# Two first pairs of the hidden folds leave the rank-2 projection for w2: five batches in place of six

## What is computed

```
xn = layernorm(x)
s  = weighted sum of shifted copies of xn (top 6 lags of each row's autocorrelation, softmax)
w1, w3: 2752 x 1024, each a 2752 x 256 matrix repeated four times along its columns; w2: 1024 x 2752, 1024 x 688 repeated likewise
gate = silu(xn w1' + 0.5 (xn a1') b1')      a1, b1 ... of rank 2
up   =      xn w3' + 0.5 (xn a3') b3'
hid  = gate * up                            4096 x 2752
y    = hid w2' + 0.5 (hid a2') b2'          a2: 2 x 2752, b2: 1024 x 2
out  = x + s * silu(y)
```

## Time and profile before

| | before |
|---|---|
| median of 3 runs | 848.47 us (848.42 to 848.81) |
| the profiled execution | 847.11 us, of which the span is 845.3 us |
| PE busy | 828.8 us, 98% of the span |
| DVE busy | 578.0 us, 68% |
| ACT busy | 332.1 us, 39% |
| POOL busy | 146.4 us, 17% |
| chain that ended last, PE's share | 90% |
| mean granted TensorE clock | 0.998 |

### The profile page before, as it was taken

The page is one execution under the profiler, slowest core; times in us unless marked ns, Lnnn a source line. Parts: engine busy times, 40 slices in busy tenths (PEclk is TensorE's granted clock), DMA queues, the critical chain, the costliest instruction groups (busy, mean ns, idle before and its releaser), DMA issues.

```text
span 845.3 us, 11238 instructions
## 1 busy us (share of the span) xinstructions
PE 828.8 (98%) x4200; PEld 440.2 (52%) x4200; DVE 578.0 (68%) x941; ACT 332.1 (39%) x544; POOL 146.4 (17%) x238
## 2 busy tenths in 40 slices
PE   5999999999999999999999999999999999999997
PEld 4434575336844367434763347534575336844366
DVE  7878734686767776688667776678766686744535
ACT  5987644434133342333423333333323334122231
POOL 5233102222012220122201230023201222000000
PEclk9999999999999999999999999999999999999999
DMA  9730035000230003200041010511014000220004
GB/s 292 268 109 26 26 126 199 26 26 26 100 125 26 26 26 125 100 26 26 27 160 65 26 30 22 200 30 45 26 51 175 26 1 0 101 100 1 1 2 149
DMA packets 18903, 62.13 MB, mean 73 GB/s; under 512 B 2464, under 2 KB 4224, under 8 KB 18576
## 3 DMA queue, kind: packets, MB, share of 16 engines
q1 hardware_dynamic: 18832, 61.28, 21.0%
HBM read 44.49 MB, written 16.78 MB: 72 GB/s over the span
## 4 chain that ended last, share of the span: by engine, by line
PE 90%; DVE 3%; ACT 2%; issue 2%; DVEq 1%; DMA 1%; POOL 0%; SPq 0%; ACTq 0%; POOLq 0%
PE g L1237 26%; PE u L1237 24%; PE zb L1397 5%; PE g L1456 4%; PE u L1456 4%; PE u L1465 4%; PE g L1465 4%; PE u L1463 4%; PE g L1463 4%; PE g L1285 3%; PE mb L1322 1%; DMA xf<-in_x 1%; PE g L1459 1%; PE u L1459 1%; DVE junk L797 1%
## 5 line engine op out<-in xcount | busy, mean ns | idle before, releaser
L539 ACT ACTIVATE sil<-g,winv 128x512 f32<-128x512 f32 (+1 forms) x176 | 120.0, 683 | 267.6 <-PE g L1285 239.5
L840 DVE SCALAR_TENSOR_TENSOR h<-u,winv,sil 128x512 f32<-128x512 f32 x168 | 125.7, 749 | 121.3 <-ACT sil L539 105.9
L1237 PE MATMUL g<-xt,w_h 128*128 128x512 f16 x656 | 196.2, 381 | 0.0
L1237 PE MATMUL u<-xt,w_h 128*128 128x512 f16 x656 | 195.1, 379 | 0.0
L797 DVE CUSTOM_DVE_ANT_0 junk<-xn,abc 128x1024 bf16<-128x1024 f32 x96 | 120.3, 1253 | 6.0 <-issue 2.7
L1237 PE MATMUL u<-xt,w_l 128*128 128x512 f16 x328 | 124.3, 379 | 0.0
L1237 PE MATMUL g<-xt,w_l 128*128 128x512 f16 x328 | 124.3, 379 | 0.0
L1237 PEld LDWEIGHTS u<-xt,w_h 128*128 128x128 f16 x656 | 64.2, 98 | 77.4
L1237 PEld LDWEIGHTS g<-xt,w_h 128*128 128x128 f16 x656 | 55.5, 98 | 83.7 <-issue 32.1
L447 POOL TENSOR_TENSOR ve<-mv,three 128x1 f32<-128x1 f32 x30 | 6.1, 203 | 474.9 <-DVE mv L779 474.8
L539 ACT ACTIVATE gg<-g 128x512 f32<-128x512 f32 x32 | 19.1, 598 | 139.7 <-PE g L1459 64.1
(11 more groups left out here) (254 smaller groups left out, 1128.2 us busy)
## 6 DMA issues: line engine op xcount, KB each, us to landing
xr<-in_x SPq DMA_DIRECT2D x32, 512.0 KB, 4.7
out_x<-ob SPq DMA_DIRECT2D x31, 512.0 KB, 2.9
xf<-in_x SPq DMA_DIRECT2D x30, 512.0 KB, 3.3
raw_w<-in_w2t SPq DMA_DIRECT2D x1, 2560.0 KB
abc<-in_a SPq DMA_DIRECT2D x1, 2048.0 KB, 8.3
raw_w<-in_w1t SPq DMA_DIRECT2D x2, 768.0 KB, 7.8
raw_w<-in_w3t SPq DMA_DIRECT2D x2, 768.0 KB, 9.2
raw_w<-in_w1t SPq DMA_DIRECT2D x1, 704.0 KB, 12.5
```

Source lines behind the costliest of these rows:

```text
L539: return nc.scalar.activation(out, in_, f, **kw)
L840: stt(out=h[0:n, p % NH, :], in0=up, scalar=winv[0:n, 3 * block_of(p) + 1:3 * block_of(p) + 2], in1=sil[0:n, p % 2, :], op0=ALU.mult, op1= ...
L1237: o = mm(bank[:], a, x, start=opens and t == 0, stop=closes and t == len(terms) - 1)
```

## The change

The identity behind it: within fold n, the sum over j of a[4n+j] h[4n+j] equals a[4n] times the fold's sum plus the sum over j = 1 to 3 of (a[4n+j] - a[4n]) h[4n+j]. The first part has the form of the down projection, so 0.5 a[4n] b2 can be added to w2's rows of fold n. This is done for folds 3 and 4. Pairs 12 and 16 then drop out of the projection, 20 pairs are left, and they make five batches of four, at pairs 5, 9, 13, 19 and after the first part of the down projection.

In the first group PE makes the four products (`base_product`, two folds by two halves of 512 columns, two rows deep) in bank mb at pairs 8, 10, 15 and 18, and DVE adds each to w2 (`add_base`) at the head of the following pair. SP loads the two operands in three small transfers, POOL subtracts a[4n] from its three neighbours. The other users of mb move by a pair: the spectrum to 9 and 11, its lags to 14, the transposes to 12, 13, 16 and 17.

In the front, the first block's high parts are made in halves, the first two casts of b1 and b3 go from ACT to POOL, one bound of the second block moves ahead of a z part, and one low product of the first pair moves ahead of `z0_spread`.

```diff
--- before.py
+++ after.py
@@ -25,7 +25,9 @@
 NH = 6
-ZB = (NP_ + 3) // 4
+BASE = (3, 4)
+Z_PAIRS = tuple(p for p in range(NP_) if p not in [4 * n for n in BASE])
+ZB = len(Z_PAIRS) // 4
@@ -51,6 +53,10 @@
     return P if p < LAST else HALF_ROWS
+
+
+def batches_to(p):
+    return max(k for k, z in enumerate(Z_PAIRS) if z <= p) // 4 + 1
@@ -185,6 +191,7 @@
         raw_a2 = sb("raw_a2", [P, NP_, 2], F32)
+        base_a = sb("base_a", [2, len(BASE) * P], F32)
@@ -216,6 +223,7 @@
         a_raw = sb("a_raw", [4, L], F32, at=o_at)
+        base_b = sb("base_b", [2, L], F32, at=o_at)
@@ -278,7 +286,8 @@
         b2_zero, table_done = sem("b2_zero"), sem("table_done")
-        a2_done, zeroed = sem("a2_done"), sem("zeroed")
+        a2_done, a2_diff, zeroed = sem("a2_done"), sem("a2_diff"), sem("zeroed")
+        base_loaded, base_ready, base_done = sem("base_loaded"), sem("base_ready"), sem("base_done")
@@ -295,6 +304,8 @@
             return i * NP_ + p + 1
+        def at_high(b, m, k):
+            return 2 * m + k + 1 if b == 0 else 2 * b + m + 3
@@ -303,16 +314,18 @@
-        STATS_AT = [(3, 7, 10, 13)] + [(1, 7, 13, 19)] * (NG - 1)
-        NORM_AT = [(5, 9, 12, 16)] + [(2, 8, 14, 20)] * (NG - 1)
+        STATS_AT = [(3, 7, 10, 14)] + [(1, 7, 13, 19)] * (NG - 1)
+        NORM_AT = [(5, 10, 13, 17)] + [(2, 8, 14, 20)] * (NG - 1)
         Z_AT = [{}] + [{3 + 6 * q + r: (q, r) for q in range(3) for r in range(4)}] * (NG - 1)
-        X_AT = {3: (0, 0), 4: (0, 1), 6: (1, 0), 7: (1, 1), 11: (2, 0), 12: (2, 1), 15: (3, 0), 16: (3, 1)}
+        X_AT = {3: (0, 0), 4: (0, 1), 6: (1, 0), 7: (1, 1), 12: (2, 0), 13: (2, 1), 16: (3, 0), 17: (3, 1)}
         W2L_AT = {16: 0, 18: 1}
-        C_AT = [(8, 10)] + [(5, 9)] * (NG - 1)
-        I_AT = [(13,)] + [(11,)] * (NG - 1)
-        FAR_AT = [(8, 11, 14, 18)] + [(4, 10, 16)] * (NG - 1)
+        C_AT = [(9, 11)] + [(5, 9)] * (NG - 1)
+        I_AT = [(14,)] + [(11,)] * (NG - 1)
+        FAR_AT = [(8, 12, 16, 20)] + [(4, 10, 16)] * (NG - 1)
         FAR0_AT = (5, 6, 7, 9)
-        FLAG_AT = [18] + [18] * (NG - 1)
+        BASE_AT = {8: (0, 0), 10: (0, 1), 15: (1, 0), 18: (1, 1)}
+        Z2_AT = {5: 0, 9: 1, 13: 2, 19: 3}
+        FLAG_AT = [20] + [18] * (NG - 1)
@@ -336,7 +349,7 @@
         CAST_AT, STEP_AT, B_AT = {4: 0, 6: 1}, {5: 0, 7: 1}, {2: 1, 9: 2, 13: 3}
-        W2_AT = {13: 0, 15: 1, 16: 2, 18: 3, 19: 4, 20: 5}
+        W2_AT = {13: 0, 15: 1, 16: 2, 18: 3, 20: 4, 21: 5}
@@ -407,6 +420,12 @@
             front_load(1, 1)
+            sp.wait_ge(a_ready, 1)
+            sp.dma_start(base_b[:], d["w2t"][96:98, HN, :]).then_inc(base_loaded, 16)
+            for k, n in enumerate(BASE):
+                with nc.allow_non_contiguous_dma(reason="two rows of 128 numbers"):
+                    sp.dma_start(base_a[:, k * P:(k + 1) * P],
+                                 d["a2t"][:, 4 * n, :].rearrange("p r -> r p")).then_inc(base_loaded, 16)
@@ -514,10 +533,21 @@
             last_spread()
+            for k in range(2):
+                pairs = slice(0, BLOCK[2] // 2)
+                if k:
+                    pool.wait_ge(b_rest_done, 1)
+                else:
+                    pool.wait_ge(b_loaded, 16 * 11)
+                cp(b_part[:, pairs, :], raw_b[:, pairs, :]).then_inc(b_part_done, 1)
...
             pool.wait_ge(c_loaded, 16 * 3)
+            for n in BASE:
+                tt(raw_a2[:, 4 * n + 1:4 * n + 4, :], raw_a2[:, 4 * n + 1:4 * n + 4, :],
+                   raw_a2[:, 4 * n:4 * n + 1, :].broadcast_to([P, 3, 2]), ALU.subtract).then_inc(a2_diff, 1)
+            pool.wait_ge(a2_diff, len(BASE))
@@ -635,21 +665,24 @@
-            def w_high(b, m):
+            def w_high(b, m, k=0):
...
                 act.wait_ge(wscl_done, min(b, 2) + 1)
+                if b == 0:
+                    A(wt_h[m][:, k, lo:hi], raw_w[b][:, m, k, :], scale=s).then_inc(wh_done, 1)
+                    return
...
-            def b_cast(n, k):
-                pairs = (slice(0, BLOCK[2] // 2), slice(BLOCK[2] // 2, NP_ // 2))[n]
+            def b_cast(k):
+                pairs = slice(BLOCK[2] // 2, NP_ // 2)
                 if k:
-                    act.wait_ge(b_rest_done, 2 * n + 1)
-                elif n == 0:
-                    act.wait_ge(b_loaded, 16 * 11)
+                    act.wait_ge(b_rest_done, 3)
+                else:
+                    act.wait_ge(b_part_done, 2)
@@ -684,6 +717,8 @@
                 act.wait_ge(wl_done, 12 if n < 3 else 16)
+                if n in BASE:
+                    act.wait_ge(base_done, 2 * BASE.index(n) + 2)
@@ -700,22 +735,22 @@
             x_copy(1, 1)
-            w_high(0, 0)
+            w_high(0, 0, 0)
...
             quarter_normal(3)
+            w_high(0, 0, 1)
...
             xt_high(0, 1)
+            w_high(0, 1, 0)
...
             A(rsb[:], mb[:], ACT.Copy).then_inc(rsb_done, 1)
-            w_high(0, 1)
-            b_cast(0, 0)
+            w_high(0, 1, 1)
...
             A(z_part[0][:], mb[:], ACT.Copy).then_inc(z0_part, 1)
-            b_cast(0, 1)
+            w_bound(1, 1)
...
             A(z_part[1][:], z_rest[:], ACT.Copy).then_inc(z0_part, 1)
-            w_bound(1, 1)
@@ -731,7 +766,7 @@
                         if p in CAST_AT:
-                            b_cast(1, CAST_AT[p])
+                            b_cast(CAST_AT[p])
@@ -816,6 +851,13 @@
+            def add_base(k, half):
+                n, c = BASE[k], slice(HALF * half, HALF * half + HALF)
+                dve.wait_ge(base_ready, 2 * k + half + 1)
+                dve.wait_ge(w2_loaded, 16 * 7)
+                stt(out=raw_w2[:, n, c], in0=mb[:], scalar=0.5, in1=raw_w2[:, n, c], op0=ALU.mult,
+                    op1=ALU.add).then_inc(base_done, 1)
+
@@ -833,7 +875,7 @@
                 if p >= NH:
-                    dve.wait_ge(z2_done, at_group(i, ZB, (p - NH) // 4 + 1))
+                    dve.wait_ge(z2_done, at_group(i, ZB, batches_to(p - NH)))
@@ -1064,7 +1106,7 @@
                 lo, hi = block_cols(b)
-                dve.wait_ge(wh_done, 2 * b + m + 1)
+                dve.wait_ge(wh_done, at_high(b, m, k))
@@ -1130,10 +1172,10 @@
             xt_low(0, 1)
+            w_low(0, 1, 0)
...
             tt(zc[:], zb[:], rsb[:], ALU.mult).then_inc(zc_done, 1)
-            w_low(0, 1, 0)
@@ -1152,6 +1194,8 @@
                         lag_gap(0)
+                    if i == 0 and p - 1 in BASE_AT:
+                        add_base(*BASE_AT[p - 1])
@@ -1240,8 +1284,8 @@
                 b, c = BLOCK.index(p), pair_col(p)
-                pe.wait_ge(wh_done, 2 * b + m + 1)
                 for k in range(2):
+                    pe.wait_ge(wh_done, at_high(b, m, k))
@@ -1263,7 +1307,10 @@
                 if p == 0:
+                    lower(0)
                     z0_spread()
+                    lower(1)
+                    return
@@ -1314,7 +1361,7 @@
                 if i == 0:
-                    pe.wait_ge(x1_done, 4)
+                    pe.wait_ge(base_done, c + 1)
@@ -1332,7 +1379,20 @@
+            def base_product(k, half):
+                if k:
+                    pe.wait_ge(gap_done, 1)
+                    pe.wait_ge(x1_done, (6, 8)[half])
+                else:
+                    pe.wait_ge(x1_done, 4)
+                    pe.wait_ge(sq_done, half)
+                pe.wait_ge(base_loaded, 16 * 3)
+                mm(mb[:], base_a[:, k * P:(k + 1) * P], base_b[:, HALF * half:HALF * half + HALF], start=True,
+                   stop=True).then_inc(base_ready, 1)
+
             def flag_sum(i):
+                if i == 0:
+                    pe.wait_ge(base_done, 4)
@@ -1349,7 +1409,7 @@
                 elif n == 6:
-                    pe.wait_ge(gap_done, 1)
+                    pe.wait_ge(base_done, 3)
@@ -1384,7 +1444,7 @@
             def z2(i, n):
-                pairs = range(4 * n, min(4 * n + 4, NP_))
+                pairs = Z_PAIRS[4 * n:4 * n + 4]
@@ -1392,9 +1452,9 @@
                 pe.wait_ge(mult_done, at_pair(i, pairs[-1]))
-                for p in pairs:
-                    c = 32 * (p % 4)
-                    o = mm(zb[c:c + 6, :], a2st[:, p, :], h[:, p % NH, :], start=n == 0, stop=p + 4 >= NP_)
+                for k, p in enumerate(pairs):
+                    c = 32 * k
+                    o = mm(zb[c:c + 6, :], a2st[:, p, :], h[:, p % NH, :], start=n == 0, stop=n == ZB - 1)
@@ -1537,8 +1597,8 @@
                     up(i, p)
-                    if p % 4 == 1 and 4 < p < NP_ - 1:
-                        z2(i, p // 4 - 1)
+                    if p in Z2_AT:
+                        z2(i, Z2_AT[p])
@@ -1549,13 +1609,12 @@
                         lags(i)
+                    if i == 0 and p in BASE_AT:
+                        base_product(*BASE_AT[p])
                     if p == FLAG_AT[i]:
-                        if i == 0:
-                            pe.wait_ge(x1_done, 8)
...
                     down_high(0, range(0, 3))
-                    z2(0, ZB - 2)
@@ -1569,7 +1628,6 @@
```

(1 more changed line is left out.)

## The result

The changed kernel takes 859.3 us (858.8 to 860.68, 4 runs) beside 848.44 us (847.36 to 848.81, 4 runs) for the kernel before: ratio 1.0131, 95% interval 1.0117 to 1.0146. The forecast was 854.9 us, range 850.0 to 857.8. The sign is right, and the loss, 10.9 us where 6.4 were forecast, puts the time outside the range. The profiled execution took 859.39 us, span 857.6 us, mean clock 0.991 (before: 847.11, 845.3, 0.998). Before's profiled execution was 1.3 us faster than its median, the changed kernel's lies at its own, so the spans differ by 12.3 us and the medians by 10.9; run 1 shows what can lie between.

The account below looks back on a forecast made before the run. PE, busy 98% of the span, was taken as the bound. -6.7 - 1.3 - 1.2 + 3.9 + 9.3 + 2.4 = +6.4 us on a span of 845.3 gave 851.7, a median of 854.9 us, range 850.0 to 857.8.

Parts of the forecast that it names:

- three waits for DVE: Group 0, PE waiting for mb around pairs 9, 11 and 15: 2.9, 2.7 and 3.7 us, together +9.3 us.
- the clock: Group 0, slow PE work behind the waits: two falls in three waits at 1.2 us each, +2.4 us.
- four products: Group 0, PE's four added fp32 products of 512 columns at 0.97 us each: +3.9 us.
- the front: Before the first `lora`: two casts moved from ACT to POOL start everything earlier, -1.3 us (bounds 0.3 to 1.8).
- the old wait before 63.00: Group 0, PE's idle time before the transposes, made by a late `normalise`: it goes, -1.2 us.
- the dropped batch: Projection, one batch fewer in each of eight groups at 0.84 us: -6.7 us.
- ACT's two casts come off the path: Front: casts of b1 and b3, 0.74 us each on ACT, leave the path, 1.3 us after overlap.
- Nothing covers it and nothing takes its place: Projection: the dropped batch's 0.84 us per group is saved in full, 6.7 us in all.
- rival 4: Groups 1 to 7: product 19 comes 1.07 us later and PE feels it, up to +5, 859 us; chance 0.08.
- From the span to the median: Whole kernel: the profiled execution lies 1.4 us below the median, so 853.5 became 854.9 us.
- the third (DVE not in the way, 843.2 us): Group 0: DVE reaches the adds before PE wants mb, so waits and clock losses vanish, 843.2 us; chance 0.08.
- see no way round: Group 0: the second and third waits, 2.7 and 3.7 us, were held unavoidable because `lora` closes the even pair.

Follow-up runs that it names:

- run 1: Kernel before with only the changed kernel's front (casts on POOL, halved high parts, earlier low product), six batches, no products: 847.54 us against 848.03.
- run 2: Changed kernel with 11, 13 and 15 unread products filling PE's three long waits: 853.97 us, ratio 1.0075.
- run 7: Changed kernel with second_z0 moved behind the second half of down_high(1): 858.36 us (853.89 to 860.9), ratio 1.0109.
- run 3: Changed kernel with DVE's reads of mb at the head of their own pair, except the third product's add: 848.45 us, ratio 1.0005.
- run 5: Kernel before without its last batch in all eight groups (pairs 20 and 21 missing from the rank-2 sum): 846.25 us, ratio 0.9979.
- run 9: Run 8's kernel with the fourth batch issued behind pair 18, not 19, in groups 1 to 7: 849.05 us, ratio 1.0009.
- run 10: Run 5's kernel with the fourth tile's statistics one pair earlier in groups 1 to 7: 841.77 us, ratio 0.9925.
- run 8: Changed kernel with all mb reads first, second and fourth tiles' statistics later, w2 scaling back at pairs 18 to 20, second_z0 behind down_high(1): 843.48 us.

## Why the prediction was wrong, step by step

The terms, in us on the span. "Measured" is read from the changed kernel's profile, with run 2 as the scale for the clock.

| step | forecast | measured |
|---|---|---|
| three waits for DVE | +9.3 | +9.8 (2.87, 3.25, 3.67) |
| the clock | +2.4 | +5.7 (1.35, 1.70, 2.67) |
| wait for `rsb` | not in it | +1.4 |
| four products | +3.9 | about +3.8 |
| the front | -1.3 | -0.5 |
| the old wait before 63.00 | -1.2 | -1.2 |
| the dropped batch | -6.7 | -7.1 |
| sum | +6.4 | +11.9 (the spans: +12.3) |

The 7.1 us are the 6.3 that groups 1 to 7 gained and 0.84 for group 0, which was not measured apart. On the span the forecast missed by 5.9 us: the clock has 3.3 of them, the wait for `rsb` 1.4, the front 0.8.

- **The clock: mechanism right, size wrong by 3.3 us.** This is the step that failed. I read a ceiling for one fall off the front's sixteen transposes, 2.4 us, took half of it, and let only two of the waits have one. In the profiled execution all three had one, at 1.35, 1.70 and 2.67 us, together 5.7, and the third is over the ceiling. The mean clock of the kernel's other executions, 0.991 and 0.992, says that they lost about as much. The ceiling had no ground: the sixteen transposes show how much slow work stood at the start, not how long a fall behind a wait lasts. And the profile's clock row does not even show that start as slow. It reads 1.00 where two transposes took 0.63 us, against 0.38 later:

```profile
8.87 0.63 PE L1472 MATMUL zb<-ident,xr 128*128 128x128 f32 x2
...
10.39 0.38 PE L1472 MATMUL g<-ident,xf 128*128 128x128 f32 x2
```

```profile
8.00:9.00 1.00, 1.00 (x7) 1.00 (x6) 1.00 (x2) 0.45 (x1) 0.84 (x4) 1.00 1.02 352
```

The Trainium skill (TensorE: Matmul & The Clock Gate, section Why this matters for your kernels) warns of idle gaps between bursts beyond a certain length. I had read three falls out of it, though only the third of my waits lay clearly beyond that length, and priced them at my own 1.2 us each. The count of three is what this execution had. It is not certain: run 7's first wait, equally long, had no fall, the waits of 1.6 and 1.5 us in run 3 had none, and in run 1 the clock fell behind idle times of 1.37 and 0.53 us.
- **The waits: right** in place, cause and size (2.9, 2.7 and 3.7 forecast). The second was 0.55 longer; the low part in front of its add took 1.55 us on DVE (row of 68.09), where the same form in front of the third read took 0.64. POOL ran two sums from 67.82 to 70.23, beside the first of these, and only its small steps on the statistics beside the other; whether that is the cause no run shows.
- **The wait for `rsb`: missed.** I followed mb through the pairs and stopped at the flag. Behind them two things moved against each other. W2_AT puts w2's last two scalings one pair later, and ACT takes `zq`, the two halves of xt and then `rsb` in one run behind DVE's end of the group; `rsb` is copied at 122.97. PE, a batch short, is there 0.8 us earlier. In run 5, where the batch alone is missing and the tables are those of before, PE waits 0.2 us for `rsb`. So most of the 1.4 us comes from the moved tables; that it is W2_AT is argued, since no run puts that entry back alone. A step of the diff that I had not costed at all.
- **The front: 1.3 forecast, 0.5 measured.** POOL's cast takes 0.72 us and not 1.3 (ACT's own is 0.74 in the earlier trace rows), so the term that I was unsure of was better than I took it. What failed is "ACT's two casts come off the path". The diff shows that `w_bound(1, 1)`, 1.48 us, moves into the place of the second cast. The second `z_part` starts at 25.25 in the changed kernel, later than at 24.80 in before, and `zst` binds where b did:

```profile
17.23 0.72 POOL L542 CAST b_part<-raw_b 128x640 bf16<-128x640 f32 x1 [0.58 <-DMA raw_b<-in_b]
...
23.78 1.48 ACT L569 ACTIVATE w_sq<-raw_w 128x1536 bf16<-128x1536 f32 x1
```

- **The products: right.** From the product at 63.01 to the next `chain`, at 64.28, are 1.27 us, of which `lora`'s own share is 0.33 (58.85 to 59.18 in before). That leaves 0.94 for a product, where I took 0.97.
- **The dropped batch: the right number on a wrong reason.** "Nothing covers it and nothing takes its place" holds only because the fourth batch moved from pair 17 to 19. Runs 5, 9 and 10 show that a loop beside PE was within about 0.1 us of PE's own sum. The later batch stands behind the pair whose product the statistics follow, and so leaves the loop. In group 1 of the changed kernel the statistics of the fourth tile end at 215.99 and PE comes to the last batch at 221.20, 5.2 us later; in before it is 198.45 and 202.57, 4.1 us. I called the later batch harmless, and rival 4 even feared it. It is what makes the saving real; that my term came out within 0.4 us was luck:

```profile
215.78 0.21 DVE L814 BATCH_NORM_AGGREGATE mv<-bn 128x2 f32<-128x12 f32 x1
...
217.21 1.25 ACT L569 ACTIVATE xn<-xf,nm,rs 128x1024 f32<-128x1024 f32 x1 [0.83 <-POOL nm L471]
```

- **From the span to the median: 1.4 us that were not there.** I added to the forecast what before's profiled execution lay below its median. The changed kernel's profiled execution lies 0.1 us above its own. So the forecast of the median missed by 4.4 us, while that of the span missed by 5.9. The smaller miss is luck.

Of the rivals, the third (DVE not in the way, 843.2 us) is what run 8 made true by reordering: 843.48 us. Where I could "see no way round", run 3 put DVE's reads in front of the product that waits for `lora`, and the second and third wait went.

What stays open: why one wait of 2.9 us is followed by a fall and another one is not, why a fall behind the same wait cost 1.70 us once and 2.78 another time, what the 0.4 us is that the terms leave over, and what the `rsb` wait is worth alone.

## What to carry to other kernels

A long wait of PE can cost more than its own length, for a slow stretch may follow it: here the three waits of 9.8 us in all were followed by falls of the clock that cost 5.7. So when an edit puts a read of a shared bank into another engine's queue, place that read as far ahead in the queue as its data allow, and give each wait of some 3 us a range for the clock, from nothing to the 2.8 us seen here, and not one price. When work is taken from an engine that is busy for 98%, look for the loop beside it before counting the gain: follow one group's hand-overs round to the same instruction of the next group, and ask which side of the loop the removed work stands on. A table with an entry moved "by a pair" is an edit like any other: each one needs its row, also behind the stretch that the change is about.

## What the runs showed that I had not expected

- PE's clock fell to 1.2 GHz behind idle times of 2.87, 3.25 and 3.67 us in the midst of dense work, and stayed at 1.00 behind 1.6 and 1.5 us. The three falls cost 1.35, 1.70 and 2.67 us. Behind an idle time of 2.88 us in run 7 there was none, and behind one of 3.25 us the fall cost 2.78. In run 1 the clock fell to 0.50 behind idle times of only 1.37 and 0.53 us, where the changed kernel, with 1.57 and 0.53, kept 1.00. The 39 products of no use in the waits made the kernel 5.3 us faster.
- A cast of 128 x 640 from fp32 to bf16 takes 0.72 us on POOL and 0.74 on ACT.
- 0.98 us of PE's work moved by one pair within a group changed the time by 5.6 us over seven groups (runs 8 and 9).
